# A four-layer graph network on one core: scatter of group keys replaced by a search, branch-free gathering passes with twelve buffers

## The chip, the cores and the metric

The kernel runs on one core of one Trainium2 chip. The metric is the device time of one execution in microseconds. Engines: TensorE (PE, its weight loads PEld), VectorE (DVE), ScalarE (ACT), GpSimd (POOL), SyncE (SP).

## The reference, cut to what matters

There are 12500 nodes of 128 features and 200000 edges, sorted by `dst`. Each layer applies norm and ReLU, then a graph step, and adds the result to `x`:

```
layer 0: agg[n] = sum of edge_attr over edges with dst == n; MLP 272 -> 1024 -> 128
layer 1: attention: softmax over the edges of each dst of leaky_relu(s_src[src]+s_dst[dst]+s_rel), weighted sum
layer 2: agg_fwd = segment_sum(w * x[col], row); agg_bwd = segment_sum(w * x[row], col), w = rsqrt degrees
         out = 0.5*(agg_fwd @ W_src.T + b_src) + 0.5*(agg_bwd @ W_dst.T + b_dst)
layer 3: mean over edges of edge_weight * x[src] by dst, two matrices, norm, ReLU
```

## The kernel before, in words

`gnn` is a list of phases. Each phase gives every engine its own program; semaphores order them inside it, and a barrier ends it.

**Two orders of the edges.** The setup (`p_lists` to `p_post`) cuts the edges, sorted by `dst`, into 121 chunks of 1664 (`NCK`), and inside a chunk sorts them by the window of 128 nodes that holds their `src` (98 windows, `NW`). Runs are padded to groups of four edges. P order is by chunk and then window: 482 blocks (`NBP`) of 128 groups. Q order is by window and then chunk: 558 blocks (`NBQ`), the groups of each window padded to whole blocks. A group has a place in P and one in Q. From P to Q the kernel computes the place in `p_perm` (`GQR`) and keeps it in DRAM (`gqd`). From Q to P it uses a scatter: in `p_l0`, POOL writes for each P block the four keys of each group and its P number, five words, to row `SI` of `keyd` (L1204 to L1208, 482 indirect DMAs with twelve semaphores). `p_post` fills `keyd` with the padding key 255 first (L849) and works out `SI` (L886 to L896). `p_keys` loads `keyd` back, splits it into the keys `KQ` and the index `GP`, transposes the keys with TensorE and stores them as rows for `produce_q` (L2262 to L2288).

**Three sums over neighbours** (layer 2 forward, layer 2 backward, layer 3). Each is a produce phase and an aggregate phase.

- `produce_p` (L2429) walks P blocks. A table of 128 node rows per chunk is loaded by ScalarE's queue (L2543), split by POOL in five steps into three bf16 parts (L2476 to L2520), and for each block TensorE spreads the keys (L2621), VectorE compares (L2583), TensorE picks with twelve products (L2614), ScalarE copies (L2553), and SP stores 128 rows of 512 floats to `pbuf` (L2493). Eight buffers are used.
- `produce_q` (L2309) walks Q blocks with a table of all windows in SBUF. Per block: spread (L2405), comparison (L2395), twelve picks (L2419), copy (L2373), store to `xbuf` (L2343), six buffers. At the first of each six blocks TensorE's queue loads six table offsets from SBUF into registers (L2410). The loops of both are peeled by `peeled` (L2292).
- `aggregate` (L2643) reads the other order back: POOL gathers 128 rows per block by indirect DMA (`gather_groups`, L1188), into six slots; `edge_pass` (L949) then builds a selection of 4 x 128 columns from the keys (VectorE, L967), TensorE multiplies features by selection in four fp32 products (L1063), and VectorE adds the 128 columns to the accumulator at the block's window (L1008). A memset of one element (L1005) tells POOL that a slot is free. In layer 3, ScalarE first scales the rows by the edge weight (L1126).

`edge_pass` also serves layer 0, with windows of 48 nodes and a count. It handles a block whose nodes span more than one window by a branch and an inner loop:

```
lo, hi = get(b, s, it, last)                         # L1014
with e.If(lo + width < hi):                          # L1016
    ...
sel(e, s, kl).then_inc(oh, 1)                        # L1026
accumulate((s + 1) % 3, e.snap(wq, ...))             # L1028, block b - 2
```

`get` (`unit_ranges`) loads the ranges of six blocks into registers at once. VectorE first clears the accumulator (L973).

**Layer 0's nodes** (`l0_nodes`, L1271): 25 groups of 512 nodes. TensorE runs transposes, the MLP in fp32 (L1364, L1366, L1376), then the transposes of the group before (L1386) and its scores. The scores of `dst` are kept in row 0 of `R` (L1473) and `p_flag` stores and reloads that row (L1536).

## Time and profile before

| | us |
|---|---|
| median of 3 runs | 9336.75 (9331.7 to 9336.76) |
| the profiled execution | 9342.07 |
| its span | 9340.4 |
| PE, PEld busy | 7261.6, 5838.2 |
| DVE, ACT, POOL busy | 6413.4, 3252.4, 4037.3 |
| granted TensorE clock, mean | 0.881 |

Three views are used. The table of stages cuts the span at given times and gives, for each stage, its length, the busy time and number of instructions of each engine, the granted TensorE clock as a share of full speed, the DMA engines' busy share and GB/s. The groups of instructions give for a line, engine and operation the count, busy time, mean ns of one, and the idle time before them with what ended it ("issue" where the profile shows nothing that was waited for). The timeline gives start, length, engine, line, operation and in brackets the idle time before it. PEldq is the queue that feeds TensorE; its register and branch instructions are not counted as busy.

### The profile page before, as it was taken

The numbers are of one execution on the slowest core, as the hardware profiler recorded it, in microseconds if no ns is written. First come the engines' busy times: TensorE is split into PE (matmuls) and PEld (weight loads), VectorE is DVE, ScalarE is ACT, GpSimd is POOL, SyncE is SP. The second block draws the span as 40 slices with busy tenths as digits, with TensorE's granted clock in tenths as the row PEclk, the third lists the DMA queues.
The fourth block names the chain that finished last, engine by engine and source line by source line (L and its number), as shares of the span: only waits on it lengthen the run. The fifth ranks groups of instructions, "written<-read, shape, count | busy, mean of one in ns | idle before, by whom it ended". The sixth has DMA issues, their size and how long they took to land. (4 is left out here: it accounts for less than half of the span.)

```text
span 9340.4 us, 229910 instructions
## 1 busy us (share of the span) xinstructions
PE 7261.6 (78%) x60542; PEld 5838.2 (63%) x60851; DVE 6413.4 (69%) x20871; ACT 3252.4 (35%) x9379; POOL 4037.3 (43%) x4385
## 2 busy tenths in 40 slices
PE   4855677899968888888868977758877775886777
PEld 4855566544446666666667766646666664666665
DVE  5999888511167777777777766656666676666667
ACT  3533322222223333333235500025520025557882
POOL 2000577000057777777625567730037740006771
PEclk7975789999977777777789999989999988999997
DMA  0000466300024444444347866665556644556663
GB/s 21 2 2 1 110 140 140 91 24 24 23 73 105 107 105 106 106 105 105 91 147 271 289 183 191 191 156 230 230 199 191 192 156 178 230 230 183 184 182 106
DMA packets 645062, 1262.07 MB, mean 135 GB/s; under 512 B 126526, under 2 KB 183433, under 8 KB 644569
## 3 DMA queue, kind: packets, MB, share of 16 engines
q1 hardware_dynamic: 424337, 704.50, 23.0%
q0 software_dynamic: 199040, 544.46, 21.7%
q10 hardware_dynamic: 21452, 10.20, 0.4%
q8 instruction: 124, 2.03, 0.1%
q14 instruction: 109, 0.89, 0.0%
HBM read 780.96 MB, written 477.75 MB: 135 GB/s over the span
## 5 line engine op out<-in xcount | busy, mean ns | idle before, releaser
L1063 PE MATMUL PS<-w,GS 128*128 128x128 f32 x12176 | 1641.7, 284 | 499.9 <-DVE AREA L1008 224.2
L1063 PEld LDWEIGHTS PS<-w,GS 128*128 128x128 f32 x12176 | 1459.6, 192 | 682.3 <-DVE w L967 437.6
L1188 POOL DMA_INDIRECT GS<-xbuf,KI x964 | 1031.2, 1070 | 1759.7 <-ACTq L132 710.1
L1171 POOL DMA_INDIRECT GS<-t1d,KI x1564 | 1493.6, 955 | 488.0 <-issue 459.6
L2395 DVE TENSOR_SCALAR AREA<-PS,IP 128x512 bf16<-128x512 f32 x1116 | 837.7, 751 | 439.6 <-PE PS L2405 361.1
L967 DVE TENSOR_TENSOR w<-IO,KI 128x512 f32<-128x512 f32 (+1 forms) x1355 | 808.6, 597 | 424.6 <-issue 413.4
L2419 PE MATMUL PS<-AREA 128*128 x13392 | 961.1, 220 | 11.1 <-ACT GS L2373 1.4
L2419 PEld LDWEIGHTS PS<-AREA 128*128 128x128 bf16 x13392 | 843.8, 98 | 170.2 <-issue 49.2
L2373 ACT ACTIVATE GS<-PS 128x512 f32<-128x512 f32 x1116 | 666.3, 597 | 613.8 <-PE PS L2419 613.5
L1188 POOL DMA_INDIRECT GS<-pbuf,XR x558 | 595.3, 1067 | 209.4 <-issue 101.4
L1598 ACT ACTIVATE w<-PS,w 128x48 f32<-128x48 f32 x1564 | 341.7, 301 | 926.9 <-PE PS L1593 926.9
L1126 ACT ACTIVATE GS<-GS,XR 128x128 f32<-128x128 f32 x1928 | 603.6, 389 | 106.0 <-DMA GS<-xbuf,KI 98.3
L1063 PE MATMUL PS<-w,XR 128*128 128x128 f32 x3128 | 510.7, 313 | 165.8 <-DVE w L967 162.3
L2405 PE MATMUL PS<-AREA,ONB 128*128 128x512 bf16 x928 | 353.2, 381 | 340.2 <-issue 143.1
L1650 PE MATMUL PS<-w,XR 128*128 128x128 f32 x3128 | 586.2, 345 | 0.0
L1063 PEld LDWEIGHTS PS<-w,XR 128*128 128x128 f32 x3128 | 430.8, 214 | 205.9 <-DVE w L967 197.1
L1207 POOL DMA_INDIRECT keyd<-AREA x482 | 480.0, 996 | 178.8 <-issue 146.1
L1644 PE MATMUL PS<-w,GS 128*128 128x128 f32 x3128 | 543.2, 332 | 0.0
L1650 PEld LDWEIGHTS PS<-w,XR 128*128 128x128 f32 x3128 | 500.3, 244 | 49.2 <-issue 28.6
L1008 DVE TENSOR_TENSOR AREA<-AREA,PS 128x128 f32 (+1 forms) x1921 | 515.9, 269 | 18.0
L967 DVE TENSOR_TENSOR w<-IO,XR 128x512 f32<-128x512 f32 x558 | 388.6, 696 | 192.5 <-issue 188.3
L1644 PEld LDWEIGHTS PS<-w,GS 128*128 128x128 f32 x3128 | 514.8, 248 | 0.5
(410 smaller groups left out, 12508.2 us busy)
## 6 DMA issues: line engine op xcount, KB each, us to landing
xbuf<-GS SPq DMA_DIRECT2D x1116, 256.0 KB
XR<-in_edge_attr SPq DMA_DIRECT2D x780, 256.0 KB
pbuf<-AREA SPq DMA_DIRECT2D x482, 256.0 KB
GS<-t1d,KI POOLq DMA_INDIRECT x1564
GS<-xbuf,KI POOLq DMA_INDIRECT x964
GS<-pbuf,XR POOLq DMA_INDIRECT x558
AREA<-t2d ACTq DMA_DIRECT2D x121, 64.0 KB
keyd<-AREA POOLq DMA_INDIRECT x482
```

Source lines behind the costliest of these rows:

```text
L967: return e.tensor_tensor(SEL[s % 3], IO[:, 0:width].unsqueeze(1).to_broadcast([128, 4, width]), kl.unsqueeze(2).to_broadcast([128, 4, widt ...
L1008: i = e.tensor_tensor(ACC[:, bass.ds(wv, width)], ACC[:, bass.ds(wv, width)], PS[:, q, 0:width], ALU.add).then_inc(acc, 1)
L1063: i = e.matmul(PS[:, s % 3, 0:128], feats(s)[0:m, r, 0:D], SELW[s % 3][0:m, width * r:width * r + 128], start=(r == 0), stop=(r == 3))
L1126: i = e.activation(feats(s)[:, r, :], feats(s)[:, r, :], ACT.Copy, scale=weight[:, bass.ds(b * 4 + r, 1)])
L1171: e.indirect_dma_start(GS[0:m, s, r, 0:wide], None, table, bass.IndirectOffsetOnAxis(ap=idx[0:m, c:c + 1].bitcast(U32), axis=0)).then_inc( ...
L1188: e.indirect_dma_start(GF[:, 512 * s:512 * s + 512], None, buf, bass.IndirectOffsetOnAxis(ap=idx[:, b:b + 1].bitcast(U32), axis=0)).then_i ...
L1207: e.indirect_dma_start(keyd, bass.IndirectOffsetOnAxis(ap=SI[:, b:b + 1].bitcast(U32), axis=0), MP[:, 5 * b:5 * b + 5], None).then_inc(sc[ ...
L1644: n = e.matmul(PS[:, 4 + i, 0:128], GS[0:m, s, r, 0:D], LLW[l][0:m, WD * r:WD * r + 128], start=(r == 0), stop=(r == 3))
L1650: n = e.matmul(PS[:, 4 + i, 128:256], EA[0:m, s, r, :], LLW[l][0:m, WD * r:WD * r + 128], start=(r == 0), stop=(r == 3))
L2373: e.activation(OUT[s], PS[:, 3 + s % 3, :], ACT.Copy).then_inc(ev, 1)
L2395: e.tensor_scalar(OHT[s % 3], PS[:, s % 3, :], IP[:, 0:1], None, ALU.is_equal).then_inc(oh, 1)
L2419: i = e.matmul(PS[:, 3 + s % 3, 128 * r:128 * r + 128], OHT[s % 3][:, 128 * r:128 * r + 128], TAB[:, bass.ds(held[0][s] + 128 * k, 128)], ...
```

## The change

1. **The scatter goes.** `keyd`, `SI`, `MP` and POOL's part of `p_l0` are removed. `p_bases` computes tables of where each chunk's groups begin in Q (`QST`) and by how much P number and Q number differ (`DVT`). A new phase `p_gp` turns them into two tables per Q block. Beside layer 0's nodes, VectorE compares all 128 places of 23 blocks at a time with the chunks' beginnings, and TensorE sums the differences of the chunks begun, one product a block. The result is the index `gpd`.
2. **Keys travel with the rows.** A row of `pbuf` has 516 floats, the last four being the keys; VectorE copies them in `produce_p`. A row at the end of `pbuf` holds zeros and keys 255, for the places that no group fills. `p_keys` runs after layer 2 forward and loads no `keyd`; ScalarE saves the gathered keys in the aggregate phase.
3. **`sum_pass` replaces `edge_pass`** for the three sums. It has no branch for wide blocks: the Q blocks are never wide, and for P blocks one flag (`FLP`) chooses between a fast program and a general one. Twelve slots (`GRING`), no one-element memset; windows for twelve blocks are loaded as three or four words.
4. **`produce_q`** loads its offsets packed three to a word, once in eighteen blocks.
5. `l0_nodes` stores each group's scores to `sdf` itself, so `p_flag` only loads them.

```diff
     def p_l0():
-        sc = [p.sem(f"sc{i}") for i in range(12)]
-        @p.on("gpsimd")
-        def _(e):
-            for b in range(NBP):
-                if b >= 12:
-                    e.wait_ge(sc[b % 12], 16 * (b // 12))
-                e.indirect_dma_start(keyd, bass.IndirectOffsetOnAxis(ap=SI[:, b:b + 1].bitcast(U32), axis=0),
-                                     MP[:, 5 * b:5 * b + 5], None).then_inc(sc[b % 12], 16)
...
     l0_nodes, tensor, after mlp(g):
+            def places(g):
+                e.wait_ge(th, g + 1)
+                if g >= BE_:
+                    e.wait_ge(eg, g // BE_)
+                for k, b in enumerate(lot(g)):
+                    o = 3 * (b - BG * (g - g % BE_))
+                    i = e.matmul(PS[:, 4, o:o + 3], TH[g % 2][0:GPM, k, :], DB[0:GPM, :, b], start=True, stop=True,
+                                 skip_group_check=True)
     l0_nodes, vector: compare(0), compare(1) ahead of the loop, compare(g + 1) after post(g)
+                    e.tensor_tensor(TH[g % 2][0:GPM, 0:k, :].rearrange("p b (a d) -> p b a d", d=2),
+                                    IOB[0:GPM]..., QBD[0:GPM, v[0]:v[0] + k, :]..., ALU.is_ge).then_inc(th, 1)
...
     gather_groups:
-                if b >= UN:
-                    e.wait_ge(bd, b - UN + 3)
+                if b >= GRING:
+                    e.wait_ge(bd, b - GRING + 3)
+                    if kept:
+                        e.wait_ge(kept, b - GRING + 1)
...
     sum_pass, vector (fast):
+            def add(b, q, w_):
+                e.wait_ge(bd, b + 3)
+                past(e, acc, b, 1)
+                e.tensor_tensor(ACC[:, bass.ds(w_, 128)], ACC[:, bass.ds(w_, 128)], PS[:, q, 0:128], ALU.add
+                                ).then_inc(acc, 1)
+            def step(b, s, it):
+                if inq:
+                    e.wait_ge(ready[s], it * 16 + 16)
+                sel(e, s % 3, gslot(s)[:, 4 * D:PW] if inq else keys[:, bass.ds(b * 4, 4)]).then_inc(oh, 1)
+                if s >= 2:
+                    add(b - 2, (s - 2) % 3, low[s - 2])
...
     sum_pass, tensor (fast):
+                e.wait_ge(oh, b + 1)
+                past(e, acc, b, 3)
+                for r in range(4):
+                    i = e.matmul(PS[:, s % 3, 0:128], feats(s)[:, r, :], SEL[s % 3][:, r, :], start=(r == 0), stop=(r == 3))
+                i.then_inc(bd, 1)
...
     produce_q, tensor:
-            peeled(e, NBQ, UN, step)
+            wr = [reg(e, "wr") for _ in range(UN)]
+            with e.Fori(0, NQ3) as o:
+                v = ranges(e, 3, o * UN + NBQ, UN, 128 ** 3 - 1)
+                for s in range(UN):
+                    e.reg_mov(wr[s], v[s])
+                with e.Fori(0, 3) as j:
+                    for s in range(UN):
+                        it = o * 3 + j + 1
+                        w_ = e.snap(((e.snap(wr[s], ...) & 127) * 384).with_bounds(max_val=384 * 97))
+                        e.reg_alu(wr[s], wr[s], 7, ALU.arith_shift_right)
+                        step(it * UN + s, s, it, w_)
...
     produce_p, vector:
+                    past(e, st[s], it, 1, 16)
+                    e.tensor_copy(OKEY[s], CMF[:, bass.ds(b * 4, 4)]).then_inc(kc, 1)
...
-    for phase in (..., p_post, p_l0, p_flag, p_l1, p_l1_nodes, p_keys, p_l2f,
+    for phase in (..., p_post, p_gp, p_l0, p_flag, p_l1, p_l1_nodes, p_l2f, p_keys,
```

## Rows read from the trace of the kernel before

**Rows 1.** Table of six stages that the change touches, columns as told above.

```profile
1768.00:2614.00 846.00, 810.54 (x2920) 395.31 (x2920) 158.32 (x677) 221.56 (x451) 0.00 (x0) 0.98 0.07 24
4907.00:5387.00 480.00, 435.89 (x6146) 374.31 (x6266) 361.76 (x482) 260.26 (x482) 247.94 (x605) 0.99 0.80 282
5387.00:6195.00 808.00, 604.47 (x4468) 537.70 (x4468) 542.65 (x1683) 0.00 (x0) 595.34 (x558) 0.98 0.68 181
6252.00:6889.00 637.00, 528.01 (x7111) 434.52 (x7206) 417.53 (x557) 330.98 (x555) 0.00 (x0) 0.99 0.59 228
6889.00:7576.00 687.00, 520.38 (x3911) 464.19 (x3908) 468.86 (x1458) 2.98 (x5) 512.02 (x482) 0.99 0.65 187
8432.00:9142.00 710.00, 523.53 (x3860) 463.23 (x3860) 468.80 (x1455) 603.61 (x1928) 519.16 (x482) 0.99 0.63 180
```

**Rows 2.** POOL's groups of instructions: forward gathering pass, then layer 1's gather.

```profile
L1188 POOL DMA_INDIRECT GS<-pbuf,XR x549 | 586.1, 1068 | 197.2 <-issue 99.6 <-DVE w L1005 97.6
...
L1171 POOL DMA_INDIRECT GS<-t1d,KI x1509 | 1441.4, 955 | 460.5 <-issue 444.1 <-PE PS L1650 16.4
```

**Rows 3.** Timeline of the forward gathering pass: start us, us, engine.

```profile
5802.45 0.96 POOL L1188 DMA_INDIRECT GS<-pbuf,XR  x1 [0.30 <-DVE w L1005]
...
5802.61 0.69 DVE L967 TENSOR_TENSOR w<-IO,XR 128x512 f32<-128x512 f32 x1
...
5803.52 0.69 DVE L967 TENSOR_TENSOR w<-IO,XR 128x512 f32<-128x512 f32 x1
...
5803.71 1.33 POOL L1188 DMA_INDIRECT GS<-pbuf,XR  x1 [0.30 <-issue]
```

**Rows 4.** TensorE's weight loads and its queue in the first produce_q pass.

```profile
6504.06 0.10 PEld L2405 LDWEIGHTS PS<-AREA,ONB 128*128 128x128 bf16 x1
...
6507.60 0.10 PEld L2405 LDWEIGHTS PS<-AREA,ONB 128*128 128x128 bf16 x1
...
6510.23 0.10 PEld L2405 LDWEIGHTS PS<-AREA,ONB 128*128 128x128 bf16 x1 [1.70 <-issue]
...
L2415 PEldq ALU_OP  x6: 32/32/36, 6503.0 to 6506.8; - x6
...
L2419 PEldq FUSED_REGOPS  x18: 46/46/46, 6503.2 to 6507.4; - x18
...
L2297 PEldq COMPARE_BRANCH  x1: 208/208/208, 6507.6 to 6507.6; - x1
```

**Rows 5.** Timeline of produce_p: table loads and POOL's first step.

```profile
5151.25 0.35 ACTq L2543 DMA_DIRECT2D AREA<-t2d  x1
...
5153.72 0.40 POOL L2478 TENSOR_TENSOR AREA<-AREA,w 128x128 bf16<-128x128 f32 x1 [1.38 <-DMA AREA<-t2d]
...
5159.05 0.35 ACTq L2543 DMA_DIRECT2D AREA<-t2d  x1
```

**Rows 6.** Accumulations of layer 0's edge pass, beside the scatter and after it.

```profile
L1008 DVE TENSOR_TENSOR AREA<-AREA,PS x315: 199/205/209, 1030.7 to 1628.5; 128x48 f32 x158
...
L1008 DVE TENSOR_TENSOR AREA<-AREA,PS x68: 203/205/207, 1635.1 to 1762.4; 128x48 f32 x68
```

**Rows 7.** Timeline of p_perm: nearest rows for the new comparisons and products.

```profile
683.53 1.02 DVE L769 TENSOR_TENSOR AREA<-IOB,AREA 128x1664 bf16<-128x1664 bf16 x1
...
684.04 0.28 PE L796 MATMUL PS<-AREA 99*128 99x3 bf16 x4
```

**Rows 8.** Timeline of p_flag: a cast beside POOL's memsets.

```profile
2635.48 9.54 DVE L1526 CAST w<-w 8x1579 bf16<-8x1579 f32 x1
```

**Rows 9.** Timeline of p_bases: one of its chained steps.

```profile
671.02 0.26 DVE L681 SCALAR_TENSOR_TENSOR w<-w 121x98 f32<-121x98 f32 x1
```

**Rows 10.** Timeline of p_keys: the copy of the reloaded keys.

```profile
4884.67 1.32 DVE L2273 COPY XR<-AREA 128x2232 f32<-128x2232 f32 x1 [15.40 <-DMA KI<-gqd]
```

**Rows 11.** Timeline at the start of the forward gathering pass.

```profile
5409.05 0.95 POOL L1188 DMA_INDIRECT GS<-pbuf,XR  x1 [12.23 <-DVE w L1005]
```

**Rows 12.** The backward gathering pass's DMAs: ns min/median/max, first and last start.

```profile
L1188 POOL DMA_INDIRECT GS<-xbuf,KI x482: 951/957/1472, 6896.5 to 7566.7; - x161
```

497 lines of the change are left out of this document (381 added, 116 removed).

## The prediction

> **What bounds the kernel now.** I read the table of stages first, because seventeen phases run one after another with a barrier between them, so a saving counts only in its own stage. [rows 1] shows those that the change touches. What is added lies in the setup before layer 0 and in the nodes of layer 0; what is removed lies in layer 0's edge pass and the reload of keys; what is reshaped are one produce_p pass (480 us), two produce_q passes (637 us, and the second alike) and three gathering passes (808, 687, 710 us).
>
> Then each loop's limiter, from the groups of instructions, the timeline and the waits.
>
> Gathering passes: POOL is the bound, though page and table show it busy only 73%. Every indirect DMA is followed by 0.30 us in which POOL starts nothing [rows 2, 3], waiting or not. Over the steady part of layer 2's forward pass 549 DMAs took 586.1 us and 197.2 us lay between them, of which 549 x 0.30 = 165 is that gap; only some 32 us is real waiting [rows 2]. A DMA takes 0.96 us, or up to 1.44. The long ones are those that start while VectorE builds its selection: at 5803.71 the DMA starts 0.19 us into the comparison of 5803.52 and takes 1.33, longer by what is left of the comparison (0.50) less 0.13; at 5802.45 it starts first and takes 0.96 [rows 3]. So the mean is 1.068 here, and 0.955 in layer 1's gather, where no such 512-wide comparison runs [rows 2]. VectorE and TensorE are busy 543 and 604 of 808 us [rows 1] and would fit into less; their pauses, while they load ranges, are mostly hidden by POOL.
>
> produce_q: TensorE. Blocks follow each other every 0.885 us (6504.06 to 6507.60 is four), then the weight loads pause 1.70 us before the next six [rows 4]. 637/558 = 1.142 a block, so a turn of six costs 6 x (1.142 - 0.885) = 1.54 us extra. TensorE's queue loads six ranges there, some 2.4 us from the branch at 6507.6 to the next weight load, of which the array still has work for 0.8; the branch itself is 0.21 [rows 4]. produce_p has such branches but no such loads, and TensorE works 436 of its 480 us [rows 1], with no such pause.
>
> produce_p: a ring through several engines. A table load (5151.25 to 5153.72), five POOL steps of 0.40, two blocks of picks and their copies, then the next load into that buffer at 5159.05: 7.8 us for two chunks [rows 5].
>
> Layer 0's nodes: TensorE, 810.5 of 846 us busy at granted clock 0.98 [rows 1].
>
> **The change, part by part**, against the profiled 9342 us, 5 above the median.
>
> Scatter removed (482 DMAs in layer 0's edge pass). With it 315 accumulations took 1030.7 to 1628.5, 1.904 us each; once it had ended, 68 took 1635.1 to 1762.4, 1.900 [rows 6]. That is 1 us for the pass: VectorE's own row is the bound, and the scatter lay beside it. I take 0. The Trainium skill (SBUF — State Buffer, "Who interferes with whom") says a VectorE instruction with two SBUF inputs contends with a GpSimd one that reads SBUF; on that rule alone the removal would give more, and the rows say it gives nothing here, though the same rule does fit the collisions of [rows 3].
>
> Places beside layer 0's nodes. 558 products of 123x128 weights with three columns; the nearest row is four such in 0.28 us [rows 7], 0.07 each: 558 x 0.07 = +39 us, on the bounding engine, nothing to hide behind (below 20, if half of them fall into its short waits for VectorE; above 56, if each takes the 0.10 of a weight load [rows 4]). VectorE's 25 comparisons of 2944 columns, by 1.02 us for 1664 [rows 7], are 1.8 us each, 45 in all; it is busy 158 of 846, so hidden except the first two before the first norm, with a memset: +5. The extra store of each group and the final index store go beside the slow store of the degrees: +2. The flag phase then lacks one DMA hop, but a cast of 1579 columns takes 9.54 us there, since POOL's memsets run beside it [rows 8], so those set the phase's end: 0. Price +46.
>
> Setup. p_bases gains some 25 short chained VectorE steps and three transposes; the present ones take 0.26 for 98 columns and start 0.3 apart [rows 9]: 25 x 0.28 = +7. p_gp is a new phase: barrier 2, four products about 3, nine steps of 558 columns at 0.5 to 0.7: +11. The constant phase waits for one more DMA: +2. p_post loses ten steps and gains a 968 KB store: 0. Together +20, between 12 and 30. The new index list is loaded again before the forward gather, 2 us, counted there.
>
> p_keys. It needn't reload 1.4 MB and copy it before its transposes. VectorE idles 15.40 us for the load and copies 1.32 [rows 10]; some 5 of these are the barrier and stay, as do the transposes and the row store. I take -12, between -9 and -15.
>
> produce_p with keys. VectorE gets a small copy per block, SP a second wait, rows grow from 2048 to 2064 bytes. VectorE has 0.75 of 1.0 used; the copy is 0.06 to 0.16 and meets POOL's five steps of 0.40 in half the blocks. It also waits for the store of eight blocks before, earlier than ScalarE did. Nothing shows the store's latency here. Below 0; above, every copy (0.16 + 0.20) is added to the ring's half of blocks, 482 x 0.17 = +80. I take +20, nearer the lower end as VectorE has slack. DMA is 0.80 busy [rows 1].
>
> The Trainium skill (DMA: Bandwidth & Descriptors, "How a descriptor splits into AXI transactions") says that a descriptor not starting on 256 bytes costs extra beats. Rows of 2064 bytes never stay aligned; by its rule I estimate 64 beats become up to 73, so produce_p's DMA share would go from 0.80 to 0.91, still under 1. No row here shows it; the sum doesn't use it.
>
> Gathering passes. Twelve slots instead of six: today the first block waits for a 10.6 us memset and POOL stands still for 12.23 us before its seventh DMA [rows 11]; twelve DMAs are 15 us, so this goes. So do the remaining waits of 20 to 25 us a pass. The loop's VectorE work loses memset, branch and most range loads; that was hidden. What stays is POOL: 0.957 + 0.30 = 1.26 plus the collisions. Selection runs 0.63 of 1.33 us. If its phase were random the mean delay would be 0.47 x 0.56/2 = 0.13; but a late DMA also delays the selections that it feeds, which moves them out of the way, so I take 0.07, between 0 and 0.14. A second wait in the forward pass adds 0.03 (0 to 0.06, a queue's semaphore step). Pace 1.36 forward and 1.33 otherwise, plus 8 us of tail as today (the last DMA of the backward pass starts at 7566.7 [rows 12], its stage ends at 7576):
> forward 558 x 1.36 + 2 + 8 = 769 against 805 of the stage's 808: -36.
> backward 482 x 1.33 + 8 = 649 against 677 (687 without the 7.5 before 6896.5 [rows 12] and 2.5 of the next barrier): -28.
> layer 3 649 against 708 of its 710: -59; ScalarE's scaling, 603.6 us for 482 blocks [rows 1], is 1.25 a block and stays below 1.33.
> Sum -123; at 0 collisions -230, at 0.14 about -16.
>
> produce_q, two passes. Range loads come once in 18 blocks instead of six. With array pace kept that is (0.885 x 18 + 1.7)/18 = 0.98: -91 a pass. But each block gets a mask with multiply, a shift and a register copy in TensorE's queue. That queue now takes 0.76 a block (6503.0 to 6506.8 for five) [rows 4], with three register steps of 0.046. Three more make 0.90, arithmetic of two nested counters perhaps 0.95, a branch of 0.3 per six 0.05: the queue passes the array and the 2.4 us load is no longer covered, 0.13. So about 1.06 between these steps and the array's floor: 558 x 0.08 = -45 each, -90. Ends: -91 and +20 a pass.
>
> Sum: +46 + 20 - 12 + 20 - 123 - 90 = -139. 9342 - 139 = 9203, less 5 for the median: **9198**.
>
> **Rivals.**
> - *TensorE's queue keeps ahead*: produce_q at 0.98. For: its lead of 0.8 us at the end of a turn (its queue is at the branch at 6507.6, when the array starts the turn's last twelve products). 9198 - 92 = 9106.
> - *POOL collides at random or worse*, so twelve slots buy only the starts: gathers -16 instead of -123: 9305. For: selection takes half of the time. Against: the feedback above.
> - *Key copy and stores on the ring*: produce_p +100 instead of +20: 9278.
> - *Slower: register work in TensorE's queue.* If masks and nested counters cost 0.5 us a block, produce_q goes at 1.25: +60 each instead of -45, total +71: 9408. It decides from 1.20 a block on. Against: the six register steps I count are 0.28.
> - That the scatter's removal is itself the gain (the change doing what its name says): excluded by [rows 6] to 1 us; no case of its own.
>
> **How the numbers follow.** Forecast 0.48, queue ahead 0.22, collisions 0.13, ring 0.10, slower rival 0.07. The range, 9070 to 9310, takes in the first four and half the bounds of the forecast's terms; the two ends left out are both favourable terms together, and the slower rival. 0.2% is 19 us, what a measurement can tell from no change. Faster 0.85 (the collision and ring cases count in most part), within 0.06, slower 0.09.
>
> **What would show it.** Right: layer 0's edge pass still 1.90 a block; its nodes 886 to 895 us; POOL's gaps all 0.30 and no wait after the start; mean DMA 1.00 to 1.05; produce_q 580 to 600 us a pass with a pause each 18 blocks. Wrong: a DMA of 2064-byte rows above 0.96 at its minimum (then POOL works by more than rows); waits of POOL on VectorE in mid-pass; produce_q's blocks 1.2 apart; produce_p above 520.

## The result, and the profile after

The changed kernel takes 9515.6 us (median of 4 runs, 9500.2 to 9524.1) against 9334.5 for the kernel before on the same chip: a ratio of 1.0192, interval 1.0175 to 1.021. It is slower by 181 us. The forecast was 9198 with a range from 9070 to 9310; its slower rival, register work in TensorE's queue, gave 9408.

The same table of stages as in [rows 1], from the changed kernel: layer 0's nodes, produce_p, forward gather, first produce_q, backward gather, layer 3's gather.

```profile
1777.00:2659.00 882.00, 833.37 (x3525) 415.40 (x3523) 206.59 (x758) 223.53 (x459) 0.61 (x1) 0.97 0.08 25
...
4907.00:5412.00 505.00, 459.86 (x6266) 374.85 (x6266) 412.20 (x964) 265.38 (x482) 248.45 (x605) 0.99 0.77 270
5415.00:6232.00 817.00, 631.83 (x4464) 538.50 (x4464) 505.99 (x1118) 114.57 (x558) 618.90 (x558) 0.99 0.69 181
6305.00:7029.00 724.00, 636.62 (x7254) 479.26 (x7254) 418.85 (x558) 333.17 (x559) 0.00 (x0) 0.94 0.53 203
7029.00:7694.00 665.00, 538.59 (x3856) 466.22 (x3856) 442.25 (x966) 0.00 (x0) 511.05 (x482) 0.99 0.66 190
...
8634.00:9310.00 676.00, 554.05 (x3856) 466.62 (x3856) 443.27 (x965) 603.67 (x1928) 520.76 (x482) 0.99 0.65 189
```

Two rows stand out. produce_q takes 724 us and not 637, and there are two such passes. The forward gather takes 817 and not 808, though it has lost its pause at the start. From each stage's first to its last instruction, in both traces (us):

| stage | before | after | difference | forecast |
|---|---|---|---|---|
| start to layer 0's first load | 1006.4 | 1029.6 | +23 | +20 |
| layer 0's edge pass | 760.4 | 755.0 | -5 | 0 |
| layer 0's nodes | 859.8 | 881.5 | +22 | +46 |
| layer 1 | 1991.4 | 1979.8 | -12 | 0 |
| p_keys with its barrier | 27.6 | 14.8 | -13 | -12 |
| produce_p, to the first gather | 486.4 | 511.8 | +25 | +20 |
| forward gather, to the last sum | 804.8 | 816.8 | +12 | -36 |
| backward gather | 676.9 | 664.5 | -12 | -28 |
| layer 3's gather | 708.1 | 675.8 | -32 | -59 |
| produce_q, to the next gather, twice | 699.6, 700.8 | 780.0, 781.5 | +161 | -90 |

The differences sum to 169 of the 171.6 by which the span grew. Layer 1 was not touched; it took 1977.6 in another run of the kernel before (b_noscatter, below), so its 12 us are the profile's own spread.

TensorE's queue in produce_q, the line by its operation. First 500 us of the kernel before, in which 437 blocks ran (the ALU_OP of L2415 is one a block), then 500 us of the changed kernel, with 385 blocks.

```profile
L2419 PEldq FUSED_REGOPS  x1308: 46/46/46, 6300.4 to 6799.7; - x187
...
L2415 PEldq ALU_OP  x437: 32/32/36, 6300.2 to 6800.0; - x146
```

```profile
L2553 PEldq FUSED_REGOPS  x1158: 46/46/65, 6400.0 to 6899.6; - x193
L2553 PEldq ALU_OP  x385: 36/36/36, 6400.9 to 6899.3; - x193
...
L2574 PEldq ALU_OP  x386: 36/36/36, 6400.5 to 6899.9; - x193
L2549 PEldq ALU_OP  x385: 36/36/36, 6400.7 to 6899.1; - x193
...
L2573 PEldq MOVE  x322: 29/29/29, 6400.4 to 6899.8; - x161
```

The mask (L2549 or L2553), the shift (L2574) and the copy (L2573) of the unpacking are there, each 0.03 to 0.06 us long. Counting all kinds, the queue ran 7.0 instructions a block before (3055 for 437) and 10.0 after (3858 for 385). How close they stand, in a stretch of 1.1 us of the changed kernel, is the point:

```profile
L2573 PEldq MOVE  x1: 29/29/29, 6600.7 to 6600.7; - x1
...
L2549 PEldq ALU_OP  x1: 36/36/36, 6601.0 to 6601.0; - x1
...
L2553 PEldq FUSED_REGOPS  x3: 46/46/60, 6601.3 to 6601.6; - x3
```

The three FUSED_REGOPS are 46 to 60 ns long but begin about 0.13 us apart; in this trace the short ones take 0.09 to 0.10 us from start to start, some up to 0.17. The step of a queue is its spacing, not its length. The spacings give the block directly. From the first queue instruction of one block to that of the next, the kernel before takes 0.74 us with six instructions and 0.87 with seven, just under the 0.885 that the array needs. The changed kernel takes 1.04 with nine, 1.16 with ten and 1.60 with twelve, a branch among them.

The table's other hint is a granted clock of 0.94 in produce_q where it was 0.99. A block whose queue waits for a load takes 3.1 to 4.1 us, and behind it two or three blocks often run at the lower of the two levels (1.2 GHz), at 1.5 to 1.75 us each. From one load to the next, eighteen blocks later, it is 22.5 or 22.6 us in 11 of the 12 turns without such blocks, and 22.6 to 24.7, in the mean 23.5, in the turns with them. At 22.6 the 31 turns of a pass make 701 of its 718 us from the first comparison to the last. So the clock is worth some 20 us a pass, by this estimate, and the queue the other 60.

POOL's gathers, by the line's own rows. First the forward pass of the changed kernel, then the backward pass:

```profile
L1269 POOL DMA_INDIRECT GS<-pbuf,XR x282: 947/1102/1472, 5415.0 to 6211.4; - x141
L1269 POOL DMA_INDIRECT AREA<-pbuf,XR x276: 949/1123/1466, 5422.7 to 6201.9; - x138
...
L1269 POOL DMA_INDIRECT GS<-xbuf,KI x242: 947/954/1472, 7029.3 to 7687.8; - x121
L1269 POOL DMA_INDIRECT AREA<-xbuf,KI x240: 949/956/1457, 7036.8 to 7684.7; - x120
```

The gaps went nearly as forecast: they average 0.32 and 0.31 us (0.36 and 0.33 before). But the median gather of the forward pass is now 1.11 us, where it was 0.957, as in the backward pass [rows 12]. In the kernel before some 31% of the gathers took over 1.0 us, now 66% in the forward pass, 39% in the backward one, 50% in layer 3. The timeline of the forward pass, VectorE's comparisons (L2829) and POOL's gathers, shows how (start us, us):

```profile
5803.98 0.69 DVE L2829 TENSOR_TENSOR w<-IO,AREA 128x512 f32<-128x512 f32 x1 [0.62 <-DMA AREA<-pbuf,XR]
...
5804.30 1.20 POOL L1269 DMA_INDIRECT AREA<-pbuf,XR  x1 [0.30 <-ACT XR L2972]
...
5805.34 0.69 DVE L2829 TENSOR_TENSOR w<-IO,AREA 128x512 f32<-128x512 f32 x1 [0.47 <-DMA AREA<-pbuf,XR]
...
5805.81 1.05 POOL L1269 DMA_INDIRECT AREA<-pbuf,XR  x1 [0.30 <-ACT XR L2972]
...
5806.69 0.69 DVE L2829 TENSOR_TENSOR w<-IO,AREA 128x512 f32<-128x512 f32 x1 [0.46 <-DMA AREA<-pbuf,XR]
...
5807.16 1.04 POOL L1269 DMA_INDIRECT GS<-pbuf,XR  x1 [0.30 <-ACT XR L2972]
```

Each gather shown starts inside a comparison and is longer by the comparison's remainder less 0.13, the rule of [rows 3]: 5804.30 has 0.37 left and takes 1.20; 5805.81 and 5807.16 have 0.22 left and take 1.05 and 1.04. And each comparison waits for a landing. Over the pass up to its last 50 blocks (5415 to 6134), this is what ended VectorE's idle time before the 500 comparisons on record (us, times):

```profile
  DMA AREA<-pbuf,XR: 131.7, 222
  DMA GS<-pbuf,XR: 127.2, 222
```

By these traces that is the change's own doing: the keys now travel with the row, so a comparison can't start before its row has landed, 3.6 to 4.3 us after the gather's start. 460 of the 558 gathers (82%) start inside a comparison, where chance would give about half (0.69 of 1.43 us) and the kernel before had 45%. The offset isn't fixed, though: it goes from 0 to 0.69 us within the pass. The backward pass, whose keys lie in SBUF, has 53% (40% before), layer 3 67% (39% before). No run parts the keys from the rows again, so this reading rests on the traces alone.

### The profile page after: what moved, and what is told of

Same layout as the page of the kernel before. It is cut to its first block and busy times, and to the rows that moved or that the text cites. A ratio compares the mean times of both kernels' runs of the same rounds, so it can differ in the third digit from the quotient of the medians.

```text
span 9511.9 us, 226670 instructions
## 1 busy us (share of the span) xinstructions
PE 7597.6 (80%) x61407; PEld 5949.3 (63%) x61408; DVE 6427.8 (68%) x19865; ACT 3370.4 (35%) x9937; POOL 3568.5 (38%) x3902
## 5 line engine op out<-in xcount | busy, mean ns | idle before, releaser
L1269 POOL DMA_INDIRECT GS<-xbuf,KI x484 | 523.6, 1082 | 1755.4 <-ACTq L137 816.9
L2553 PE MATMUL PS<-AREA 128*128 x13392 | 1120.2, 229 | 7.3
L2553 PEld LDWEIGHTS PS<-AREA 128*128 128x128 bf16 x13392 | 896.8, 102 | 292.8 <-issue 212.5
L2889 PE MATMUL PS<-w,GS 128*128 128x128 f32 x6128 | 871.1, 287 | 247.3 <-DVE w L2829 139.0
L2889 PE MATMUL PS<-w,AREA 128*128 128x128 f32 x6048 | 856.8, 286 | 199.4 <-DVE w L2829 81.3
L2889 PEld LDWEIGHTS PS<-w,GS 128*128 128x128 f32 x6128 | 743.0, 192 | 374.3 <-issue 188.5
L2889 PEld LDWEIGHTS PS<-w,AREA 128*128 128x128 f32 x6048 | 729.4, 191 | 325.5 <-DVE w L2829 156.0
L2829 DVE TENSOR_TENSOR w<-IO,KI 128x512 f32<-128x512 f32 x964 | 662.7, 688 | 70.9 <-issue 69.0
L2542 PE MATMUL PS<-AREA,ONB 128*128 128x512 bf16 x1116 | 450.4, 404 | 302.6 <-issue 144.9
L2859 DVE TENSOR_TENSOR AREA<-AREA,PS 128x128 f32 x1522 | 434.2, 285 | 381.4 <-PE PS L2889 376.6
L1269 POOL DMA_INDIRECT AREA<-xbuf,KI x480 | 508.2, 1059 | 146.3 <-issue 109.1
L1790 PE MATMUL PS<-w,GS 128*128 128x128 f32 x3128 | 544.7, 332 | 0.0
L1790 PEld LDWEIGHTS PS<-w,GS 128*128 128x128 f32 x3128 | 515.7, 248 | 1.1 <-issue 0.3
L2776 PE MATMUL PS<-AREA 128*128 128x128 bf16 x5784 | 405.8, 220 | 22.0 <-POOL AREA L2677 19.5
```

The costliest lines, as they stand in the source:

```text
L1269: e.indirect_dma_start(gslot(s)[:, 0:m], None, buf, bass.IndirectOffsetOnAxis(ap=idx[:, b:b + 1].bitcast(U32), axis=0)).then_inc(ready[s], 16)
L1790: n = e.matmul(PS[:, 4 + i, 0:128], GS[0:m, s, r, 0:D], LLW[l][0:m, WD * r:WD * r + 128], start=(r == 0), stop=(r == 3))
L2542: e.matmul(PS[:, s % 3, :], ONB[:], RW[:, s, :], start=True, stop=True).then_inc(kb, 1)
L2553: i = e.matmul(PS[:, 3 + s % 3, 128 * r:128 * r + 128], OHT[s % 3][:, 128 * r:128 * r + 128], TAB[:, bass.ds(w_ + 128 * k, 128)], start=(k ...
L2829: return e.tensor_tensor(SEL[q][:], IO[:].unsqueeze(1).to_broadcast([128, 4, 128]), kl.unsqueeze(2).to_broadcast([128, 4, 128]), ALU.is_equal)
L2859: e.tensor_tensor(ACC[:, bass.ds(w_, 128)], ACC[:, bass.ds(w_, 128)], PS[:, q, 0:128], ALU.add).then_inc(acc, 1)
```

## The experiments

Times are medians; ratios are to the kernel before, run on the same chip beside them. The runs fell on chips of two kinds. On the result's own chip and on the one that the record numbers 7 the kernel before takes 9335 to 9344 us; "the first chip" stands for both below. On numbers 12, 15, 14 and 11 it takes 10650 to 10671; "the second chip" stands for these four.

### What slows produce_q

**q_old** puts back TensorE's old loop; **b_newq** gives the kernel before the new one.

```diff
 q_old, produce_q, tensor:
-            alone(0)
-            wr = [reg(e, "wr") for _ in range(UN)]
-            with e.Fori(0, NQ3) as o: ...
+            def step(b, s, it):
+                if s == 0:
+                    held[0] = ranges(e, 3, it * UN, UN, 384 * 97)
+            peeled(e, NBQ, UN, step)
```

> The changed kernel, with TensorE's part of produce_q as it was before: one load of six offsets a turn of six blocks, no packed words, no inner loop, no register work of unpacking. Theory (the queue's register work): in the changed kernel a block of produce_q takes 1.15 us where no load stands, against 0.885 before, with 10.0 instructions of TensorE's queue a block against 7.0. Then each produce_q goes back from about 718 to 637 us (first to last comparison), the whole falls by 161, to 9354 +- 10, and what is left against the kernel before (about +20) is the rest of the change. Rival (something else in the changed kernel slows produce_q, such as the index rows read from another place, or the clock): each pass stays above 690 and the whole above 9450.

> The kernel before, with the packed offsets alone: produce_q's TensorE part of the changed kernel, and the packing in p_bases that it needs. Theory (queue's register work): each produce_q goes from 637 to about 718 us, and the whole from 9335 to 9495 +- 15. Rival (the slowing needs the rest of the change): below 9400, and the forecast's own price, -45 a pass, would give 9250.

Both ran on the second chip. q_old: 9970.3, ratio 0.9345 (0.933 to 0.9361); produce_q 694.4 and 696.8 us, first to last instruction, against 777.5 and 775.6 of the unchanged changed kernel there (696.2 and 697.3 in the kernel before on the first chip). b_newq: 10841.6, ratio 1.0158 (1.0141 to 1.0175), that is +170 us; expected was +160. So the new loop alone costs 79 to 85 us a pass, in either kernel. The absolute times expected were those of the first chip; the differences held.

**q_unrolled** keeps the packed words but writes the eighteen blocks out; **q_shift** writes them out and keeps the moving registers; **q_dose** and **q_dose2** add register work to the old loop.

```diff
 q_unrolled (q_shift has the same loops, with wr, its copy and its shift kept)
-                with e.Fori(0, 3) as j:
+                for j in range(3):
                     for s in range(UN):
-                        w_ = e.snap(((e.snap(wr[s], ...) & 127) * 384)...)
-                        e.reg_alu(wr[s], wr[s], 7, ALU.arith_shift_right)
+                        w_ = e.snap((((v[s] >> 7 * j if j else v[s]) & 127) * 384)...)
 q_dose, on q_old's loop            q_dose2, on q_old's loop
+ for _ in range(3):               + for _ in range(2):
+   e.reg_alu(dm, dm, 1, ALU.mult) +   w_ = e.snap((((w_ >> 7) & 511) * 128)...)
```

> The changed kernel, with the packed offsets kept (one load of six words in eighteen blocks), but the eighteen blocks written out: no inner loop, and no moving register that is shifted each time; a block's offset is made from its word with a shift by a constant, a mask and a multiplication. Theory (the queue's register work, about 0.09 us for each added queue instruction beyond what the matmuls hide): queue instructions fall from 10.0 to about 8.5 a block and the block from 1.15 to between 0.90 and 1.03, each pass from 718 to 560 to 640 and the whole to 9200 to 9360. Rival (the load itself, or the longer pause after it in which the clock falls, makes the loss): a block stays at 1.15 without the load, and the whole above 9450.

> The changed kernel, with the eighteen blocks written out (no inner loop), but with the moving registers kept: each word is copied to a register and shifted after each use. It stands between the changed kernel (produce_q 777 us, 10.0 queue instructions a block) and the one written out with constant shifts (654 to 660 us, 8.1 a block). Theory of the count: the inner loop's compare, branch and addition are 0.5 instructions a block and one of 0.2 us in six blocks, and copying 0.33: 9.1 to 9.6 a block, 1.00 to 1.08 us a block, produce_q 680 to 735. Rival (the inner loop alone is the loss, its branch or its fetch): produce_q falls to 655 to 665.

> The changed kernel with TensorE's part of produce_q as it was before, and three register operations added to each block (a register multiplied by one), which nothing reads. Theory (what slows a block is the number of instructions in TensorE's queue, 7.0 a block before and 10.0 in the changed kernel): with 10.0 again and the old loads, a block where no load stands takes 1.10 to 1.18 us and not 0.885, and since the load of six stays each turn, a pass takes 637 + 558*0.25 = about 775 us from first to last comparison (718 in the changed kernel, 637 with the old loads). Rival (it is the unpacking's dependence, a register that the next matmul's address waits for, or the inner loop, not the count): the added operations are independent of the addresses, so a block stays at 0.89 and a pass at 637 to 660.

> The changed kernel with TensorE's part of produce_q as it was before (one load of six offsets a turn), but each offset goes twice through a shift by 7 to the right, a mask and a multiplication by 128, which leave it as it is: this repeats the dose run, whose three added operations nothing read and the compiler dropped (its queue still had 7.2 instructions a block and a block took 0.89). Theory (each instruction in TensorE's queue costs 0.09 to 0.14 us there, and once their sum passes the 0.885 us of the matmuls, the queue sets the block): 11 to 12 instructions a block, a block where no load stands 1.1 to 1.3 us, and produce_q from 697 to about 820 to 900 us. Rival (the inner loop or the moving register of the changed kernel): a block stays at 0.89 to 0.95, and produce_q below 730.

q_dose's added operations are not in the queue's record (7.2 instructions a block), so that run says nothing of their price: 9991.9, ratio 0.9367, produce_q as in q_old but for 3 to 5 us. The others, with the mean block over 480 us of the first pass from the count of row spreads (L2542), such as these of q_unrolled and of q_dose2:

```profile
L2542 PE MATMUL PS<-AREA,ONB x452: 378/380/635, 6899.6 to 7379.5; 128*128 128x512 bf16 x151
```

```profile
L2542 PE MATMUL PS<-AREA,ONB x309: 376/379/634, 6899.9 to 7379.9; 128*128 128x512 bf16 x155
```

| kernel | queue instructions a block | loads in 18 blocks | mean block, us | produce_q, us | ratio |
|---|---|---|---|---|---|
| q_old | 7.0 | 3 | 480/421 = 1.14 | 694, 697 | 0.9345 |
| q_unrolled | 8.1 | 1 | 480/452 = 1.06 | 654, 660 | 0.9269 |
| q_shift | 9.1 | 1 | 480/414 = 1.16 | 706, 714 | 0.9370 |
| changed kernel | 10.0 | 1 | 480/371 = 1.29 | 777, 776 | 0.9499 |
| q_dose2 | 11.0 | 3 | 480/309 = 1.55 | 928, 930 | 0.9784 |

With one load in 18, a block costs 0.10 us more for the ninth instruction in the queue, and from there to the tenth 0.13 for 0.9 of an instruction, which includes the inner loop's branch and part of the lower clock. Between loads without blocks at the lower clock, eighteen blocks take 18.5 or 19.4 us in q_unrolled, 20.3 in most turns of q_shift and 22.5 in the changed kernel, so the order stays without the clock. From the first comparison to the last q_unrolled's passes take 595 and 599 us, within the 560 to 640 expected. q_dose2 has the loads of q_old and four instructions more, and is slower by 0.41 a block, 0.10 each; its 928 is a little above the 820 to 900 expected. The rival, the inner loop alone, falls: q_shift has none and stays 50 us above q_unrolled. So the count of the queue's instructions sets the block, once their spacing passes the 0.885 us that the array needs; and a load once in 18 blocks is a gain, if the unpacking costs one instruction and not three. Of the kinds added, only their common count was tested, not each kind by itself.

### What makes the gathers long

**iota_psum** lets the comparison read its ramp from PSUM.

```diff
 sum_pass, vector:
-            return e.tensor_tensor(SEL[q][:], IO[:].unsqueeze(1)...
+            return e.tensor_tensor(SEL[q][:], PS[:, 7, 0:128].unsqueeze(1)...
...
+            e.tensor_copy(PS[:, 7, 0:128], IO[:]).then_inc(dv, 1)
```

> The changed kernel, where the comparison SEL of the three gathering passes reads its ramp 0 to 127 from PSUM instead of from SBUF (one copy a pass puts it there); nothing else differs. Theory (the gather of POOL is held up where it is issued within a VectorE operation that reads two tensors of SBUF): with one operand in PSUM the gathers take 0.957 us at the median and in the mean (now 1.109, 1.060 and 1.080), the pitch falls from 1.43, 1.37 and 1.39 to about 1.27, and the three passes lose 558*0.15 + 482*0.10 + 482*0.12 = 84 + 48 + 58 = 190 us, less some 20 where the end of the forward pass is bound by its transfers: 9345 +- 30. Rival (the long gathers come from the transfers or from POOL itself, and the overlap with SEL is chance): means stay at 1.06 to 1.11, and the whole stays at 9515 +- 10. Second rival (VectorE's comparison gets slower with a PSUM operand, or waits): its 0.69 us would have to pass 0.9 before it binds.

It ran on the second chip: 10133.5, ratio 0.9494 (0.9478 to 0.951), no gain against 0.9499. Yet the gathers fell to 0.952 in the mean, in all three passes. The forward pass, the changed kernel (after_again) and then iota_psum, both on that chip:

```profile
L1269 POOL DMA_INDIRECT GS<-pbuf,XR x282: 947/954/1470, 5878.0 to 6715.2; - x141
...
  PE PS L2889: 92.0, 133
```

```profile
L1269 POOL DMA_INDIRECT GS<-pbuf,XR x282: 947/953/1056, 5875.0 to 6712.9; - x141
...
  PE PS L2889: 172.3, 145
```

What the gathers lost, POOL then waited for free slots (172.3 us against 92.0): on this chip the ring fills, and something behind the gathers sets the pace, 1.50 us a block in the forward pass. The packets themselves hardly differ (236 ns in the mean from 6000 to 6500 us, 230 on the first chip from 5500 to 6000), so it isn't their own time. Half of each theory held, the cause of the length and not its price there. The price on the first chip came with **best2_again**, the combined version told below. Its forward pass there, to be set against the 1102 and 1123 of the changed kernel:

```profile
L1269 POOL DMA_INDIRECT GS<-pbuf,XR x282: 949/953/1056, 5407.0 to 6107.4; - x141
L1269 POOL DMA_INDIRECT AREA<-pbuf,XR x276: 949/953/966, 5414.6 to 6099.9; - x138
```

And a collision that no longer delays, in its timeline: the gather starts 0.02 us into the comparison, whose operand is now "PS".

```profile
5805.66 0.69 DVE L2827 TENSOR_TENSOR w<-PS,GS 128x512 f32<-128x512 f32 x1
...
5805.68 0.95 POOL L1269 DMA_INDIRECT GS<-pbuf,XR  x1 [0.30 <-issue]
```

The pitch is 1.26 us in all three passes, which take 706.7, 613.0 and 613.8 us from the first gather to the last sum, not 816.8, 664.5 and 675.8. The comparison itself takes 0.69 us as before. The Trainium skill (SBUF — State Buffer, "Who interferes with whom") says that a VectorE instruction with two inputs in SBUF contends with a GpSimd instruction that reads SBUF; the trace agrees: with two such inputs 66% of the forward gathers take over 1.0 us, with one of the two in PSUM the longest of all takes 1.056.

**ring6** holds POOL to six gathers ahead in the changed kernel.

```diff
 gather_groups:
-                if b >= GRING:
-                    e.wait_ge(bd, b - GRING + 3)
+                if b >= 6:
+                    e.wait_ge(bd, b - 6 + 3)
... (the wait on kept likewise)
```

> The changed kernel with twelve slots still, but POOL allowed only six gathers ahead, as in the kernel before. Theory (the ring buys only the start of a pass, where the wide memset of the sums holds VectorE and POOL's gaps average 0.63 us over 40 blocks in the kernel before, 0.35 and 0.31 in the changed one): each pass gets 8 to 15 us longer on a chip where POOL sets the pace; on the second chip, where the transfers come in uneven order, perhaps 0 to 30 a pass more. Rival (twelve slots matter all through the pass): over 30 us a pass, over 90 in all.

First chip: 9545.7, ratio 1.0207 (1.019 to 1.0223). By the ratios that is 14 us more than the changed kernel, and the intervals overlap. From the first gather to the last sum the three passes take 822.1, 690.9 and 687.5 us in the profile, +5, +26 and +12; but the profiled execution was the slowest of the four (9555 us, the others from 9520), so the sum of 43 is an upper reading. Either way the ring is worth about what was expected of the start, and not over 90. The backward pass's 26 is more than the start explains; its gathers are longer as well (1.10 us in the mean, against 1.06), which would fit another phase between the two loops. That wasn't tested.

### The slow end of the forward pass

In the last 50 blocks of the changed kernel's forward pass the gathers land late. The rows on landings, for the middle (5500 to 6000) and for the end (6134 to 6213):

```profile
DMA to landing us min/median/max: 3.6/3.8/4.3
...
DMA to landing us min/median/max: 10.8/17.1/18.2
```

**pads_spread** gives the places without a group 128 rows, not one.

```diff
-    pbuf = dram("pbuf", (128 * NBP + 1, PW))
+    pbuf = dram("pbuf", (128 * NBP + 128, PW))
...
-            link(e.tensor_scalar(GSM, GSM, float(128 * NBP), None, ALU.min))
+            link(e.tensor_scalar(LIM[:], IP[:], float(128 * NBP), None, ALU.add))
+            link(e.tensor_scalar(GSM, GSM, LIM[:, 0:1], None, ALU.min))
```

> The changed kernel with 128 rows at the end of pbuf for the places that no group fills, a row of its own for each partition, instead of one row for all; nothing else differs. In the last 58 blocks of the forward pass the gathers land 15 us after their issue, not 4, the pitch is 1.6 instead of 1.43, and the sum ends 19 us after POOL's last gather. Theory (these blocks hold only such places, and 128 reads of one row are slow where 128 rows are not): landings stay at 4 us to the end, the forward pass (sum_pass, first to last instruction, 817 us in the changed kernel on the first chip, 859 on the second) loses 15 to 30 us. Rival (the end is slow for another reason): no change beyond 3 us. On the second chip the transfers set the pace all through, so a gain may be spread otherwise.

Second chip: 10107.6, ratio 0.9487 (0.9473 to 0.9502) against 0.9499, whose intervals overlap; the forward pass 848.6 against 858.7, -10. That alone would be thin. **b_noscatter** (told for its main purpose below) makes every block such a block:

```diff
 b_noscatter, p_l0 of the kernel before:
-            for b in range(NBP):
-                e.indirect_dma_start(keyd, bass.IndirectOffsetOnAxis(ap=SI[:, b:b + 1]...
```

> The kernel before without POOL's scatter in layer 0 and nothing in its place: the keys and indices by place stay as they were filled (keys 255, index 0), so the sum of layer 2 forward reads row 0 of pbuf in all 558 blocks and adds nothing, the keys that produce_q looks up are 255, and the output isn't the reference's. Theory for the second chip (the scatter starves SyncE's loads of the attributes there, 3 loads in 100 us beside it and 53 after it): layer 0's edge pass goes from 1380 to 755 us. Rival (this chip's edge pass is slow for another reason): it stays above 1200. On the first chip the edge pass has 53 loads in 100 us with the scatter too: no change there, 755 to 765. Side reading for the rows without a group: if 128 reads of one row are slow, the forward gathers, all of one row here, take 1.6 us or more a block (now about 1.43 to 1.58 with rows of their own) and the pass 890 or more; if not, about 800 to 860.

It ran on the first chip: 9472.9, ratio 1.0138 (1.0122 to 1.0154). Its edge pass and its forward pass:

```profile
1006.00:1766.00 760.00, 581.90 (x4700) 488.94 (x4700) 614.72 (x4311) 231.71 (x783) 0.00 (x0) 0.89 0.48 136
5374.00:6323.00 949.00, 637.33 (x4468) 552.12 (x4468) 562.52 (x1682) 0.00 (x0) 594.04 (x558) 0.98 0.91 154
```

The edge pass is 760 us without the scatter, as with it. The forward pass, all of row 0, takes 949 us, 1.69 a block, at a DMA share of 0.91 for 154 GB/s, where [rows 1] has 0.68 for 181. In the middle of it a packet of 4096 bytes (two rows; 5600 to 6100 us) took 377 ns in the mean, against 226 in the kernel before (5500 to 6000 us). So 128 reads of one row are slow. In best2_again, which has the spread rows, the gathers of the end land after 3.7 to 3.9 us on the first chip.

### Layer 0's nodes, and produce_p

**no_places** leaves out the comparisons, products and sums; **no_keycopy** VectorE's copy and SyncE's wait for it.

```diff
 no_places, l0_nodes:                       no_keycopy, produce_p:
-  i = e.matmul(PS[:, 4, o:o + 3], ...)      -  e.wait_ge(kc, b + 1)
-  e.tensor_tensor(TH..., ALU.is_ge)         -  e.tensor_copy(OKEY[s], CMF[:, bass.ds(b * 4, 4)])
-  e.tensor_reduce(GSM[:, a:z], ...)
```

> The changed kernel without the places work beside layer 0's nodes: VectorE's comparisons, TensorE's products of three columns and the sums of them are left out, and each place takes its own number as its index, so the gathers of layer 2 forward read other rows (that pass is not to be compared) and the output isn't the reference's. Theory (this work costs the nodes stage all that it grew by): the stage from the first node instruction to the last goes from 881.5 back to 860 us. The forecast's own price of the work was 46, of which 22 came. Rival (the growth is that of the stores of the scores, not of the places): the stage stays at 875 to 882.

> The changed kernel without VectorE's copy of four keys into each row of produce_p and without SyncE's wait for it: the key columns hold 255, so layer 2 forward adds nothing and the output isn't the reference's. produce_p took 482 us before and 505 in the changed kernel. Theory (the copy and its second wait cost the 23 us): 482 to 486. Rival (the rows of 2064 bytes cost them): 500 to 506, and the keys' copy is free.

no_places, second chip: 10124.0, ratio 0.9492; the nodes 862.2 us against 879.3, with TensorE busy 816 and not 832. The work costs 17 of the 22 us by which the stage grew. The products' own row, in the changed kernel; each is 0.164 us long, but in most pairs the next starts 0.025 us later:

```profile
L1495 PE MATMUL PS<-AREA x558: 164/164/178, 1832.3 to 2637.5; 123*128 123x3 bf16 x186
```

no_keycopy, first chip: 9508.3, ratio 1.0169 (1.0153 to 1.0185); produce_p takes 508 us from first to last engine instruction, where the changed kernel takes 505. VectorE's row shows that the copies are gone (x482 and 361.76 us, as in [rows 1]), and the stage has not moved:

```profile
4907.00:5411.00 504.00, 460.85 (x6266) 373.50 (x6264) 361.76 (x482) 265.33 (x482) 247.36 (x604) 0.99 0.78 270
```

So the theory falls: the copy is free. The trace shows where the time went. The stage is still the ring of [rows 5], and its table load now lands later (changed kernel):

```profile
5152.05 0.35 ACTq L2700 DMA_DIRECT2D AREA<-t2d  x1
5154.87 0.40 POOL L2633 TENSOR_TENSOR AREA<-AREA,w 128x128 bf16<-128x128 f32 x1 [2.09 <-DMA AREA<-t2d]
```

From the issue of a table load to POOL's first step on it, the mean of all 121 chunks was 2.44 us in the kernel before, is 2.85 in the changed one and 2.89 in no_keycopy. The rest of the turn stayed (5.37 us before, 5.31 and 5.33 now). 0.41 us in each turn of two chunks makes 25 us, the whole growth. The load's packets of 512 bytes take 35 ns in the mean where they took 27. A store packet takes 90 ns with 2064 bytes and 91 with 2048, so the stores' own packets are not slower. The rows' length is what is left that differs between the kernels beside these loads; rows stored without their last 16 bytes weren't tried, so this cause is argued, not shown.

### Why the ratio depends on the chip

> The changed kernel itself, unchanged, timed once more beside the kernel before and beside the other runs of this group, since the chip of the first group ran the kernel before in 10671 us and not in 9335. If this group's chip runs the kernel before in about 9335, theory: 9516 +- 15, ratio 1.019. If it runs it in about 10671, then layer 0's edge pass with the scatter takes 1380 us there (754 without) and the changed kernel comes to the time of the run with the old loads plus 165, that is 10135 and a ratio of 0.950. Rival: the ratio is about 1.02 on any chip, and the first group's runs differ for another reason.

The changed kernel, on the second chip: 10134.1, ratio 0.9499 (0.9483 to 0.9515). What was expected for this chip held to 1 us. There the change is 5% faster. **b_best_nosc** is the kernel before with its two gains of the next part and without the scatter; it ran on that chip too.

> The same without POOL's scatter, for the case that this group's chip is the second one; keys and indices by place stay as filled, so layer 2 forward reads row 0 in all blocks, and the output isn't the reference's. Second chip: layer 0's edge pass, first to last instruction, goes from 1380 to 755 us. First chip: 755 to 761 with and without it, and only the forward pass of one row (942 us from first to last gather with the ramp in SBUF) is of interest: if the transfers of one row hold it and not the gathers' length, it stays at 930 to 945; if the length did, it falls by 558*0.1 = 56.

10044.8, ratio 0.9424 (0.941 to 0.9437), its twin with the scatter (b_best) 10591.6. Layer 0's edge pass, with the scatter and without it:

```profile
1010.00:2390.00 1380.00, 603.93 (x4700) 505.09 (x4700) 620.60 (x4314) 227.32 (x783) 495.17 (x482) 0.70 0.27 76
```

```profile
1008.00:1772.00 764.00, 587.99 (x4700) 493.19 (x4700) 619.44 (x4310) 230.91 (x783) 0.00 (x0) 0.88 0.46 136
```

SyncE's loads of the attributes from 1100 to 1600 us, while the scatter runs, of b_newq on the second chip and of the kernel before on the first:

```profile
L1156 SPq DMA_DIRECT2D XR<-in_edge_attr x15: 332/333/333, 1117.6 to 1588.0; - x15
```

```profile
L1143 SPq DMA_DIRECT2D XR<-in_edge_attr x263: 332/333/333, 1101.6 to 1599.5; - x132
```

Fifteen loads against 263, with the same scatter beside them. The DMA engines were not busy: their share was 0.07 in b_newq from 1010 to 1660 us. So on the second chip the scatter of 20-byte rows keeps the other queue's loads from being served, and its removal is worth 615 us; on the first it is worth nothing. How the scatter holds the loads back, and whether the chips themselves differ or something around them, is open. The passes with gathers are slower there too, in every kernel (layer 1 takes 2420 to 2441 us, not 1976 to 1991).

### The best version

**best_kmaj** has the ramp in PSUM and produce_q written out, with offsets premultiplied by 128. **best2** adds the spread rows; **best2_again** is the same once more. **b_best** is the kernel before with the first two.

```diff
 best_kmaj, produce_q (and the ramp of iota_psum):
-        tv = TAB.rearrange("n (w k f) -> n w k f", k=3, f=128)
+        tv = TAB.rearrange("n (k w f) -> n w k f", k=3, f=128)
+                        w_ = e.snap(((v[s] >> 7 * j if j else v[s]) & 127 * 128)...)
-                                     TAB[:, bass.ds(w_ + 128 * k, 128)], ...
+                                     TAB[:, bass.ds(w_ + 128 * 98 * k, 128)], ...
```

> The changed kernel with two edits: the comparison SEL of the gathering passes reads its ramp from PSUM; and produce_q's eighteen blocks are written out with packed offsets that come premultiplied by 128, for a table that lies with its three parts one after the other, so that an offset is a shift and a mask, no multiplication. Theory of the queue: 7.2 instructions a block, 0.89 to 0.94 us a block and 590 to 640 us a pass from first to last comparison incl. its loads (718 changed, 637 before). Theory of the shared port: all gathers take 0.95 us; on a chip where POOL sets the pace (the kernel before at 9335) the three passes lose 84 + 48 + 58 = 190 less some 20, and the whole comes to 9516 - 2*100 - 170 = 9150 +- 50; on a chip where the transfers set the pace (the kernel before at 10671) the passes stay as they are, and the whole comes to 10135 - 200 - 2*15 = 9900 +- 50. Rival (the gathers' length is not VectorE's doing): no gain in the passes on either chip.

> The three gains together: the ramp in PSUM, produce_q written out with premultiplied offsets, and the spread rows for empty places. On a chip where the kernel before takes 9335 us: 9516 - 200 (produce_q, 100 each) - 170 (passes) - 20 = 9126 +- 50, faster than both. On a chip where it takes 10670: 9885 (measured for the first two together) less 15 to 30: 9860 +- 15. Rival: nothing beyond 9885, if the spread rows do nothing.

> The three gains together once more, for the case that this group's chip is the first one (the kernel before at 9335), where it hasn't been measured: 9126 +- 50, faster than both, with every gather at 0.95 us and the three passes about 170 us shorter than in the changed kernel (817, 662 and 674 us there), since POOL sets the pace on that chip. Rival: the passes' pace falls only to where the transfers hold it, 1.35 us a block or more, and the whole stays above 9250. On the second chip: 9859 +- 15, as measured.

> The kernel before with the two gains that don't need the change: the ramp of the comparisons SEL in the three gathering passes read from PSUM, and produce_q written out with premultiplied packed offsets (with the packing in p_bases). The scatter, the keys by place and the ring of six slots stay. Theory for the first chip (the kernel before at 9340): produce_q -40 each as in the run with all gains, the three gathering passes at 1.26 us a block and not 1.43, 1.39 and 1.46, some 10 us a pass at the start and 15 at the end of the forward pass not gained: -80 -60 -85, together 9340 - 80 - 225 + 3 = 9040 +- 40, level with the changed kernel with all gains (9035), so that the rest of the change is worth about nothing there. Rival (the old sum's waits hold the passes once the gathers are short): 9150 to 9250. On the second chip (10670): -80 and nothing in the passes, 10590 +- 30, far above 9859, because of the scatter.

Second chip: best_kmaj 9884.9, ratio 0.9264 (0.9249 to 0.928); best2 9858.6, 0.9256 (0.9243 to 0.9269); b_best 10591.6, 0.9933 (0.9921 to 0.9945), as expected. The premultiplied offsets bring nothing that q_unrolled (0.9269) hadn't; the queue still runs 8.1 instructions a block, so the multiplication had cost none of its own.

First chip: best2_again **9035.1**, ratio 0.9671 (0.9657 to 0.9685), faster than the kernel before by 309 us and than the changed kernel by 480; it is 91 below what was expected, outside the +-50. Its stages: forward gather, first produce_q from the first comparison, backward gather.

```profile
5404.00:6114.00 710.00, 618.83 (x4464) 536.47 (x4464) 503.18 (x1119) 114.59 (x558) 531.69 (x558) 0.99 0.73 208
6177.00:6777.00 600.00, 535.67 (x7254) 447.18 (x7254) 424.84 (x569) 341.00 (x573) 0.00 (x0) 0.98 0.64 246
6777.00:7390.00 613.00, 528.67 (x3856) 464.12 (x3856) 438.35 (x966) 0.00 (x0) 459.20 (x482) 0.99 0.71 206
```

b_best wasn't measured on the first chip, so how much of the 309 us needs the change at all is open there. On the second chip nearly all comes from it: 0.9256 against 0.9933.

## Why the prediction was wrong

- *produce_q, -45 a pass forecast, +81 measured.* This is the step that decides: 251 us of the 308 by which the sum of the table's terms (-139 against +169) misses. The text said "Three more make 0.90, arithmetic of two nested counters perhaps 0.95". It counted the added instructions rightly (three) but priced each at 0.05, near the 0.046 of its length, where the runs show 0.10 to 0.15 from one count to the next. The queue's measured 0.76 for some seven instructions would have given 0.11 each, and 1.1 for ten. A second step failed beside it: its own terms add to 1.13 a block (0.95 + 0.05 + 0.13), which is -7 a pass; it took 1.06, between that and the array's floor, with no row behind the choice. The measured block is 1.29. The lower clock behind the loads, some 20 us a pass, had no term. The loads' part held: with one load in 18, q_unrolled is 37 to 40 us a pass faster than q_old. The slower rival named the mechanism and its threshold (1.20 a block) and had a chance of 0.07; its price was 60 a pass, where it measured 81.
- *Gathers, -123 forecast, -33 measured.* The gaps behaved nearly as forecast (0.32 and 0.31 in the mean). The step that failed is "a late DMA also delays the selections that it feeds, which moves them out of the way, so I take 0.07". The mean delay over 0.957 was 0.15, 0.10 and 0.12 us. The kernel before had 0.11, 0.10 and 0.12 (the 1.068 of [rows 2] is the first), so its own rows already spoke against halving it. In blocks that is 558 x 0.08 + 482 x 0.03 + 482 x 0.05, 83 us. In the forward pass the landing does steer the comparison, but into the gathers and not out of their way: 82% of them start inside one. Selection takes 0.69 us in [rows 3] and not 0.63, so the random case is 0.52 x 0.56/2, 0.15. The best version, with the operand in PSUM and the spread rows, takes 224 us less in the three passes.
- *The slow end.* It had no term. From POOL's last gather to the last sum the forward pass took 20 us, where the tail was priced at 8, because the last blocks all read one row. The kernel before had it too: of its last 52 gathers, the first 46 stood 1.70 us apart.
- *Layer 0's nodes, +46 forecast, +22 measured.* The products cost 17 us, not 39: 0.03 each. "0.07 each" is a misreading of [rows 7]: its 0.28 us run from the first start to the last end of four products that overlap, each 0.166 long. The 20 of the lower end was nearer.
- *Scatter 0, flag 0, setup +20, p_keys -12, produce_p +20*: measured -5, 0, +23, -13, +25, on this chip. The first holds for this chip alone; the scatter was excluded as a case by [rows 6], and a row of one chip couldn't show the other. produce_p's size was right by luck and its reason wrong: the key copy costs nothing, and the table loads land later.
- *Rows that start off alignment.* The Trainium skill (DMA: Bandwidth & Descriptors, "How a descriptor splits into AXI transactions") made it 0.91 of the DMA engines in produce_p by an estimate; the row has 0.77. As the stage also got longer, the engines' time is the better measure: 0.77 x 505 is 389 us, 0.80 x 480 was 384, so it grew by 1% and not by 14%. The measurement decides.
- *Of the signs named*, "mean DMA 1.00 to 1.05" was wrong (1.06 to 1.11), nodes of "886 to 895 us" too (881.5), and "produce_q's blocks 1.2 apart" is what was seen (1.15 where no load stands).

## What to carry to other kernels

Price an instruction of a queue by the distance to the next one, taken from a loop that runs without waits, and multiply by the count; in these traces its duration was mostly less than half of that. Where an indirect gather collides with a VectorE instruction that reads two operands in SBUF, look whether one of them can stand in PSUM: here a constant of 128 columns was enough. Where a change makes one loop wait for another (here the comparison for the landing of its row), don't take collisions as random, nor their present share as a guide: it went from 45% to 82% here. And read a row of several overlapping instructions by their starts, not by its length divided by their number.

## What the runs showed of the hardware that wasn't expected

- The same kernel's ratio to the kernel before is 1.019 on one chip and 0.950 on another. There a scatter by POOL of 128 rows of 20 bytes each leaves 15 loads of 256 KB in 500 us for SyncE's queue, at a DMA share of 0.07; the first chip serves 263 beside the same scatter.
- 128 reads of one row of 2048 bytes: 1.69 us a block, 377 ns a packet of two rows; of rows of their own 226 ns.
- The ramp in PSUM costs VectorE nothing: 0.69 us for 128x512 f32 from either place.
- Beside stores of 2064-byte rows, packets of 512 bytes of another queue take 35 ns in the mean; beside stores of 2048-byte rows 27.
